# Second mixture of experts: rows scattered straight into their expert's stretch during the gate, instead of seat lists and row fetches afterwards

## The reference, cut to what matters

```python
H = gelu(xf @ W1 + b1)                       # (8192, 512), xf is the normalized token
probs = softmax(H @ Wg + bg)                 # (8192, 8)
assign = argmax(probs)                       # one expert per token
for e in range(8):
    y = H @ Wd[e] + bd[e]                    # (8192, 128)
    out = out + where(assign == e, probs[:, e:e+1] * y, 0)
```

## Time and profile before

| | us |
|---|---|
| median of 3 runs | 1574.37 |
| lowest, highest | 1572.56, 1574.78 |
| the profiled execution | 1575.46 |
| its span in the profile | 1573.8 |
| busy in the span: PE, DVE, ACT, POOL | 1202.6, 868.9, 801.4, 570.9 |

### The profile page before, as it was taken

How to read it: one execution, slowest core, us unless ns; L and a number is a source line. 1 busy time by engine, 2 the same in 40 slices (tenths; PEclk the granted TensorE clock), 3 DMA queues, 4 the chain that set the end, 5 groups by cost and what they waited for, 6 DMA issues and landing times. The chain is left out here.

```text
span 1573.8 us, 28989 instructions
## 1 busy us (share of the span) xinstructions
PE 1202.6 (76%) x6574; PEld 877.9 (56%) x6577; DVE 868.9 (55%) x3806; ACT 801.4 (51%) x2213; POOL 570.9 (36%) x871
## 2 busy tenths in 40 slices
PE   2444414567946999999959999999996997587776
PEld 1223303455925999999935554455443543466665
DVE  5777899957486333355557743444445665611111
ACT  3555525411246666666627765665554664533332
POOL 3666426400001777477666200000000000167775
PEclk9999955769568899999969999999998998799999
DMA  9300000000300233333311000000000322322221
GB/s 263 104 1 1 1 1 1 1 1 1 107 0 11 77 86 88 67 84 86 85 51 46 19 1 0 0 1 0 1 0 2 79 80 54 17 64 76 77 71 45
DMA packets 86039, 68.78 MB, mean 44 GB/s; under 512 B 18678, under 2 KB 74815, under 8 KB 85964
## 3 DMA queue, kind: packets, MB, share of 16 engines
q1 hardware_dynamic: 71500, 36.45, 8.8%
q0 software_dynamic: 14464, 31.52, 7.9%
HBM read 41.68 MB, written 26.77 MB: 43 GB/s over the span
## 5 line engine op out<-in xcount | busy, mean ns | idle before, releaser
L1711 POOL DMA_INDIRECT g_Z<-z,sitter x72 | 70.6, 980 | 512.8 <-SPq L1697 482.9
L1609 ACT ACTIVATE c_H<-ps,c_b 128x128 f32<-128x128 f32 x576 | 156.4, 382 | 99.6 <-PE ps L1657 99.6
L1476 POOL DMA_INDIRECT c_Z<-z,sitter x108 | 102.8, 952 | 253.3 <-POOLq L1306 204.1
L2103 PE MATMUL ps<-BIG,w_ihT 128*128 x364 | 156.0, 578 | 3.4 <-ACTq L2116 3.4
L1657 PE MATMUL ps<-c_ZT,c_w 128*128 128x128 f32 x1152 | 144.1, 279 | 2.2 <-ACT c_ZT L1598 2.2
L1643 PE MATMUL ps<-w_dn,c_H 128*128 x1152 | 141.4, 276 | 0.8 <-ACT c_H L1609 0.8
L1657 PEld LDWEIGHTS ps<-c_ZT,c_w 128*128 128x128 f32 x1152 | 137.7, 196 | 3.0 <-ACT c_ZT L1598 3.0
L1643 PEld LDWEIGHTS ps<-w_dn,c_H 128*128 128x128 f32 x1152 | 135.4, 193 | 1.1 <-issue 1.1
L1763 ACT ACTIVATE g_H<-ps,bias_cols 128x256 f32<-128x256 f32 x144 | 60.3, 470 | 114.0 <-PE ps L1800 113.2
L2103 PEld LDWEIGHTS ps<-BIG,w_ihT 128*128 128x128 f32 x364 | 69.7, 192 | 84.7 <-issue 84.7
L2111 PE MATMUL ps<-e_hs,w_hhT 128*128 128x512 f32 (+1 forms) x256 | 110.0, 572 | 0.0
(11 more groups left out here) (513 smaller groups left out, 2760.1 us busy)
## 6 DMA issues: line engine op xcount, KB each, us to landing
y<-c_ys SPq DMA_DIRECT2D x72, 128.0 KB
z<-ZB SPq DMA_DIRECT2D x32, 256.0 KB, 2.6
z<-X SPq DMA_DIRECT2D x16, 256.0 KB, 3.8
w_up<-in_L_ffn_W_dram SPq DMA_DIRECT2D x1, 2048.0 KB
w_dn<-in_L_ffn_W_dram SPq DMA_DIRECT2D x8, 256.0 KB
w_dn<-in_L_ffn_Wd_dram SPq DMA_DIRECT2D x8, 256.0 KB
c_Z<-z,sitter POOLq DMA_INDIRECT x108, 2.5
g_Z<-z,sitter POOLq DMA_INDIRECT x72, 2.8
```

The lines of the kernel that those rows point to most:

```text
L1476: pool.indirect_dma_start(Z[t % 2][h][:, :], None, z, bass.IndirectOffsetOnAxis(ap=k.sitter[:, t * HALVES + h:t * HALVES + h + 1], axis=0) ...
L1609: act.activation(H[u][:, c, h * P:(h + 1) * P], UP[u][c // 2][:, o:o + P], ACT.Gelu, bias=b1[u][h][:, c:c + 1]).then_inc(gelu, 1)
L1711: pool.indirect_dma_start(Z[t % DEPTH][h][:, :], None, z, bass.IndirectOffsetOnAxis(ap=k.sitter[:, t * HALVES + h:t * HALVES + h + 1], axis=0)
L2103: last = pe.matmul(view(k.ps[4 * u + j], wide, lanes), k.w_ihT[:, w, :], state(i, u, s, p, wide, lanes), start=True, stop=(s == 0))
```

## The change

The seat of a token is settled while the gate still runs, and its whole row (normalized token, token, weight, and now its own number as a 258th entry) is scattered straight into a stretch of `z1` that belongs to its expert and has room for all tokens.

- `gate1` is written out for all 16 groups instead of looped. Rows are built in `k.R`, a ring of five pairs of groups (eight tiles each) that takes the place of weights which are no longer needed (`spent`). `back` and `normalized` write into it.
- Per pair of groups, DVE gets `pick` (the chosen expert of its 1024 tokens, six small operations), `add_up` (running counts per expert), `weigh` (the weight by way of a tanh on ACT instead of an exponential) and `seat` (the token's row in its expert's stretch). PE gets `rank`: eleven small bf16 matmuls that add the expert's start, the counts of earlier pairs, the earlier tiles of this pair and the earlier partitions of each tile.
- POOL issues one indirect DMA per tile (`scattered`), eight per pair, once weight and seat of the pair are there. SP no longer writes rows; at the end it writes 128 filler rows behind each expert's last row.
- `route` is gone. What the experts still need from it, the expert of each block of 128 seats and now the block's first row (`base`), is worked out at the end of the gate.
- In `experts_out` SP fetches each half by a plain DMA from the row that it loads from `base`, once both scatters of the tile that used the buffer before have landed. POOL only scatters results; the destination numbers are read from the 258th column of the fetched rows.

```diff
@@ gate1 @@
+        @block.gpsimd
+        def _(pool):
+            for q in range(PAIRS):
+                pool.wait_ge(weighted, q + 1)
+                pool.wait_ge(seated, q + 1)
+                for n in range(q * PAIR, (q + 1) * PAIR):
+                    pool.indirect_dma_start(z, bass.IndirectOffsetOnAxis(ap=k.seats[:, 0, n:n + 1], axis=0),
+                                            k.R[:, row(n), :], None, bounds_check=E * STRIDE - 1, oob_is_err=False
+                                            ).then_inc(scattered[q % RING], 16)
...
+            def pick(q):
+                of = tiles_of(q)
+                dve.wait_ge(logits_sb, 2 * q + 2)
+                link(dve.tensor_reduce(out=best[:, :], in_=k.LG[:, of, :], axis=AX.X, op=ALU.max))
+                got = link.put(tt_(tied[:, :, :], k.LG[:, of, :], best[:, :, None].to_broadcast([P, PAIR, E]), ALU.is_equal))
+                tt_(k.LG[:, of, :], k.LG[:, of, :], best[:, :, None].to_broadcast([P, PAIR, E]), ALU.subtract).then_inc(shifted, 1)
...
+            def add_up(q):
+                dve.wait_ge(marked, q + 1)
+                link(dve.tensor_reduce(out=part[:, :], in_=K16[:, tiles_of(q), :].rearrange("p t e -> p e t"), axis=AX.X, op=ALU.add))
+                link(tt_(sums[:, q + 1, :], sums[:, q, :], part[:, :], ALU.add))
+
+            def weigh(q):
+                dve.wait_ge(tanhed, q + 1)
+                link.put(dve.tensor_copy(k.R[:, rows_of_pair(q), ROW - 1].bitcast(I32), token[:, tiles_of(q)]))
+                link(ts_(tanh[:, :, :], tanh[:, :, :], -1.0, 1.0, ALU.mult, ALU.add))
+                link(dve.reciprocal(tanh[:, :, :], tanh[:, :, :]))
...
+            def seat(q):
+                dve.wait_ge(ranked, q + 1)
+                link(tt_(prod[:, :, :], RANK.rearrange("p (t e) -> p t e", e=E), K16[:, tiles_of(q), :], ALU.mult))
+                link(dve.tensor_reduce(out=pos[:, :], in_=prod[:, :, :], axis=AX.X, op=ALU.add))
+                dve.tensor_copy(k.seats[:, 0, tiles_of(q)], pos[:, :]).then_inc(seated, 1)
...
+            for g in range(GROUPS + 1):
+                if g % 2 == 0 and g >= 4:
+                    seat((g - 4) // 2)
+                if g > 0:
                     dve.wait_ge(scores, g)
...
                     dve.tensor_copy(sc[:, :], SC[:, :]).then_inc(scores_sb, 1)
+                if g < GROUPS - 1:
+                    normalized(g + 1)
+                if g % 2 and g >= 3:
+                    pick((g - 3) // 2)
+                if g < GROUPS - 3:
                     back(g + 3)
+                if g % 2 and g >= 3:
+                    add_up((g - 3) // 2)
+                if g > 0:
                     dve.wait_ge(logits, g)
+                    tt_(group_of(k.LG, g - 1), GA[:, 0:GT * E].rearrange("p (t e) -> p t e", e=E),
+                        k.b_gate1[:, None, :].to_broadcast([P, GT, E]), ALU.add).then_inc(logits_sb, 1)
+                if g % 2 == 0 and g < GROUPS - 2:
+                    scale(g // 2 + 1)
+                if g % 2 and g >= 3:
+                    weigh((g - 3) // 2)
                 link.reset()
+            pick(PAIRS - 1)
+            add_up(PAIRS - 1)
+            dve.sem_inc(counted, 1)
+            weigh(PAIRS - 1)
+            seat(PAIRS - 1)
...
+            def rank(q, biased):
+                pe.wait_ge(marked, q + 1)
+                pe.wait_ge(logits_sb, biased)
+                marks = K16[:, tiles_of(q), :].rearrange("p t e -> p (t e)")
+                pe.matmul(RANK, k.ones16[:, :], apart[:, None, :].to_broadcast([P, PAIR, E]), start=True, stop=False)
+                pe.matmul(RANK, k.ones16[:, :], sums[:, q:q + 1, :].to_broadcast([P, PAIR, E]), start=False, stop=False)
+                for n in range(PAIR):
+                    pe.matmul(RANK[:, n * E:PAIR * E], k.ones16[:, :], marks[:, 0:(PAIR - n) * E], start=False, stop=False)
+                pe.matmul(RANK, k.upper16[:, :], marks, start=False, stop=True).then_inc(ranked, 1)
...
+                if g % 2 == 0 and g >= 4:
+                    rank((g - 4) // 2, g - 1)
+                if g > 0:
                     pe.wait_ge(gelu, g * C)
@@ experts_out @@
+        @block.sync
+        def _(sp):
+            def fetch(t, b, r):
+                if not (isinstance(t, int) and t < DEPTH):
+                    sp.wait_ge(placed[b], r * (16 * HALVES))
+                for h in range(HALVES):
+                    at = sp.value_load(k.base[0:1, ds(t * HALVES + h, 1)], min_val=0, max_val=E * STRIDE)
+                    sp.dma_start(Z[b][h][:, :], z[ds(at, P), :]).then_inc(fetched[b], 16)
+            rounds(sp, fetch, NT, DEPTH, 0)
...
+            for t in range(NT):
+                b = t % DEPTH
                 pool.wait_ge(y_ready, t + 1)
                 for h in range(HALVES):
...
+                    pool.indirect_dma_start(out, bass.IndirectOffsetOnAxis(ap=Z[b][h][:, ROW - 1:ROW].bitcast(I32), axis=0),
+                                            ys[b][h][:, :], None, bounds_check=B * N - 1, oob_is_err=False
+                                            ).then_inc(placed[b], 16)
```

More of the change, by code:

```diff
@@ L991, in gate1 @@
 def gate1(nc, k, sem, z):
-    copied, lifted, added, s_sel, z_ready, turned, turned_sb, up, gelu, scores, scores_sb, logits, logits_sb, s_ex, s_exd, s_x = (
+    copied, lifted, added, s_sel, z_ready, turned, turned_sb, up, gelu, scores, scores_sb, logits, logits_sb = (
         sem(f"j_{n}") for n in
-        "copied lifted added sel z turned turned_sb up gelu scores scores_sb logits logits_sb ex exd x".split())
-    kept = [sem(f"j_kept{u}") for u in range(2)]
+        "copied lifted added sel z turned turned_sb up gelu scores scores_sb logits logits_sb".split())
@@ L1007, in gate1, with mine @@
-        block = own.enter_context(nc.Block())
+        def mine(name, shape, dtype=F32):
+            return own.enter_context(nc.sbuf_tensor(f"j_{name}", shape, dtype))
+        H = [mine(f"H{u}", [P, C, GC]) for u in range(2)]
+        sc, sel, S = mine("sc", [P, GC]), mine("sel", [P, E]), mine("S", [P, GC])
+        var, both, bits, half, root = (mine(n, [P, PAIR]) for n in ("var", "both", "bits", "half", "root"))
+        best, first, total, pos = (mine(n, [P, PAIR]) for n in ("best", "first", "total", "pos"))
@@ new lines, in gate1 @@
+        tied, tanh, prod = (mine(n, [P, PAIR, E]) for n in ("tied", "tanh", "prod"))
+        token = mine("token", [P, TILES], I32)
+        K16, sums, apart = mine("K16", [P, TILES, E], BF16), mine("sums", [P, PAIRS + 1, E], BF16), mine("apart", [P, E], BF16)
+        part, pad, stride = mine("part", [P, E]), mine("padding", [P, ROW]), mine("stride", [1, E])
+        cnt, nb, end, gap = (mine(n, [1, E]) for n in ("cnt", "nb", "end", "gap"))
+        blocks, pad_at = mine("blocks", [1, E], I32), mine("pad_at", [1, E], I32)
@@ L1058, in _ @@
                     scale(0)
[L1059 to L1066, removed]
+            normalized(0)
+            for g in range(GROUPS + 1):
+                if g % 2 == 0 and g >= 4:
+                    seat((g - 4) // 2)
+                if g > 0:
                     dve.wait_ge(scores, g)
-                    if not (isinstance(g, int) and g < 2):
+                    if g >= 2:
@@ L1102, in turn_back, with tanh_of @@
                                sequences(k.BIG, g).rearrange("h t b -> h b t"), ACT.Copy).then_inc(copied, 1)
+            def tanh_of(q):
+                act.wait_ge(shifted, q + 1)
+                if q >= 1:
+                    act.wait_ge(weighted, q)
+                act.activation(tanh[:, :, :], k.LG[:, tiles_of(q), :], ACT.Tanh, scale=0.5).then_inc(tanhed, 1)
             for g in range(3):
                 turn_back(g)
[L1107 to L1109 removed]
+            for g in range(GROUPS):
+                u = g % 2
                 act.wait_ge(turned, g + 1)
[L1111 removed]
+                if g >= 2:
                     act.wait_ge(up, (g - 1) * C)
                 act.activation(k.ZS[u][:, :], TR[:, :], ACT.Copy).then_inc(turned_sb, 1)
[L1114 removed]
+                if g < GROUPS - 3:
                     turn_back(g + 3)
@@ L1157, in step @@
                     last.then_inc(scores, 1)
-                if not end:
+                if g < GROUPS:
                     pe.wait_ge(turned_sb, g + 1)
@@ L1296, in route_choices @@
+            rank(PAIRS - 1, GROUPS)
+            pe.wait_ge(counted, 1)
+            pe.matmul(COUNT, k.ones16[:, :], sums[:, PAIRS, :], start=True, stop=True).then_inc(counted, 1)
 def route_choices(nc, k, sem):
```

294 lines of the change are left out of this document (97 added, 197 removed).

## The result

The changed kernel takes 1660.7 us (median of 4 runs, 1655.2 to 1662.7) against 1574.6 before: 1.0546 of it, 95% interval 1.0532 to 1.0560, slower by 86 us. The forecast was 1633, with a range of 1602 to 1658. The direction and the added wait came as forecast; what the wait costs was forecast too small.

What follows compares the result with a forecast made beforehand. POOL's issue of four indirect DMAs was taken to set 5.2 us a tile in the expert stage. 1575.46 + 1.4 (to the first turn, gate's +20.4 included) + 57.6 (expert stage) = 1634.5, median 1633; range 1602 to 1658.

Steps and rivals of the forecast that it cites:

- Step (1): Gate: added DVE operations and `rank` ahead of the scores cost 3.4 us more per pair, +20.4 us in all.
- The tanh: Gate: one ACT tanh a pair; its own table would mean two loads more a pair, some 5 us; nothing was counted.
- Step (2): Between gate and experts: POOL's queue of sixteen scatters ends last; first transpose at 1375.2, 1.4 us later than now.
- Step (3): Expert stage: SP's fetch waits for landed scatters, 7.05 us a tile against 5.20, +57.6 us in all.
- a way: Expert stage: path from one even turn to the next, two tiles on; 14.1 us, bounds 12.9 to 15.4, counted 16 times.
- rival B: Expert stage: clock falls in the waits, 0.8 to 1.6 us more per even turn; 1659 us, or 1646; chance 0.18.
- A: Expert stage: four buffers cover the path between turns, PE sets 4.1 us a tile; 1541 us; chance 0.05.
- C: Gate: PE hides the additions, so gate and POOL's queue end 20 us sooner; 1613 us; chance 0.14.
- D: Gate: POOL's scatters take 2 us each beside DVE, the tail grows by 11; 1644 us; chance 0.05.

Runs made afterwards that it cites:

- e4_rank: The changed kernel with the gate's rank matmuls put behind the score matmuls of the same step instead of ahead of them: 1645.2 us.
- e3_copy: The changed kernel, but VectorE copies the destination numbers beside the result, so SP's fetch waits for VectorE instead of the landed scatter: 1565.1 us, 0.9943 of before.
- e2_ring8: The changed kernel with eight row and result buffers in the expert stage instead of four, the wait for the scatter kept: 1533.0 us, 0.9733 of before.
- e1b_warm6: The changed kernel with six idle matmuls on PE ahead of each even tile's wait for its rows: 1635.0 us.
- e6_loads: The changed kernel with PE's two loads of expert numbers put ahead of its wait for the rows instead of behind the turn: 1630.9 us.

## Why the prediction was right and wrong

*Step (1), the gate: right in size and, for 13.1 of the 20.1 us, in its reason.* Pairs of 17.0 us against the 17.1 forecast, +20.1 against +20.4; `rank` waits for the odd step's logits and the scores stand behind it. Inside the pair two sizes were off in opposite ways: `rank` takes 0.5 us, not 0.9, while the clock falls in the wait (0.50 at `rank`, 0.60 from the scores on for 3.33 us) and adds some 0.9 us to the scores and 0.4 to the up projection, which the sum did not have. e4_rank shows the order to be the cause of the 13.1; what the other 7.0 are stays open, so that the sum came out so close is partly luck. The tanh, whose table was in doubt, cost no load: the trace of after has none behind 1218.5 us. In most other executions of the same gate (e3_copy, e2_ring8, e1b_warm6, e6_loads) the pairs are 17.4 us and the gate 143; the profiled execution of after was the best of its four, which is some of the 5.5 us by which the median lies above it.

*Step (2), between gate and experts: right but for one term.* The queue of sixteen scatters ends last, at 1.29 us each. The first turn came 173.1 us after the gate's start, against 168.9 forecast. I had 1.1 us for leaving the block, from the end of the seat lists in the kernel before, where POOL had issued nothing in that block. Its DRAIN alone is 5.27; SP's first fetches and their landing, with 4.5 forecast, gave part of that back (3.2 from the first issue to the turn).

*Step (3), the expert stage: the term that failed.* The wait, its place in PE's order, two tiles a way, 16 ways: all as forecast. The size of a way was 15.36 and not 14.1. That lies inside the bounds (12.9 to 15.4; by the terms given the lower one is 13.05), but the upper one stood for a slow fetch, and the cause is one that the sum left to rival B. Term by term, in the way shown above: rows landed to down 1.84 (forecast 1.95), down to bias add 3.91 (2.20), the vector operations 1.13 (1.0), both scatters' start 2.07 (2.1), landing 2.27 (2.3), SP's two fetches 2.04 (2.2), landing 2.10 (2.3). One term is off, the down projection, which the sum took at the 2.05 us that it has at a clock of 1.00 and which ran at 0.50: 1.71 us more, of which the other terms give 0.4 back. From turn 2 to turn 34 the sixteen ways took 75.6 us more than before, where 57.6 were forecast. These 18.0 us are nearly all of the 18.9 by which the expert stage is above its forecast. The 18.9, with the 4.2 us by which the first turn came late (the DRAIN), less the 2.4 of earlier stretches, are the difference between the forecast of the profiled execution (1634.5) and its time (1655.2). The other 7 us up to the median belong to no term of the sum: the profiled execution of before lay 1.1 us above the median that the forecast went by, and that of after 5.5 us below its own.

*The rivals.* B is what happened on top of the forecast, behind every wait of an even turn; I had seen its sign (2.87 us after one wait) and gave it 0.18, because another wait there left the down at 2.05 us. Both of those waits were of 0.5 us ahead of the turn and 1.4 behind it; in after the sixteen are of 3.1 to 4.7 us ahead and 1.1 to 1.4 behind, and every down projection behind one took 3.5 to 3.8 us. The half speed behind B's 1.6 us stands in none of its rows. The table by stretch of before has it inside the down of 2.87 us (clock 1.00 from 1529.44 to 1530.40, 0.50 from 1531.00 to 1532.00), and in the way of after shown above the clock is 0.50 over the whole down projection: 3.77 us, 1.82 more than the other's 1.95 at 1.00. B's upper end was 1659, one us above the end of the range, and the median is 1660.7; that the two are so close is partly luck, as B had nothing for the DRAIN and the ways account for 18.0 us, not its 26. A is refuted for four buffers. What it asked for, a fetch that does not wait for the landing, is e3_copy, with 1565.1 instead of its 1541; PE sets the pace only with eight buffers (e2_ring8, 1533.0). C is refuted: the gate grew by 20.1 us. D: a scatter takes 0.98 us beside VectorE and alone.

## What to carry to other kernels

When a buffer is freed by a later event than before, count how many tiles of the bottleneck's work lie in the new way round the ring, with what stands ahead of them in PE's order: here it was two of four, and four more buffers turned 5% slower into 3% faster. Where such a wait comes back all through a stage, read the granted clock of the work behind it from a trace before you price it: here it was 0.50 to 0.56 behind waits of 3.1 to 4.7 us, and the down projection took 3.5 to 3.8 us instead of 1.95. And put a small matmul that depends on a late vector result behind, not ahead of, big ones that don't: here that was 15.5 us.

## What was unexpected of the hardware

- Idle matmuls in a wait paid: 1661 to 1635 us with six of them a way (clock 0.78 to 1.00 between 1440 and 1520 us).
- POOL's DRAIN at the end of a block grew by 0.082 us for each scatter issued in it (5.27, 5.92 and 6.57 us for 64, 72 and 80), in blocks where POOL issued nothing else.
- Two loads of expert numbers between a turn and the matmuls that use them held PE for 1.1 to 1.4 us; with eight buffers PE shows no pause for them, and moving them ahead of the wait gave 30 us, some 7 of them by the clock.
